# Loading x in quadrant order with transfers that write all 128 partitions

## The reference

```python
xn = _layernorm(x, axis=-1)
# the network, for all 16384 tokens
s = jnp.einsum('btd,dm->btm', xn, Win) + bin_          # D = 512, M = 64
h = jax.nn.relu(s[..., None] * W1 + b1)                # 16 hidden values for each of the 64
g = jnp.einsum('btmh,mh->btm', h, W2) + b2
out = jnp.einsum('btm,md->btd', g, Wout) + bout
# the result
x = x + attention(xn, ...) + out
```

## Time and profile before

| | before |
|---|---|
| median of 3 runs | 382.41 us |
| the three runs | 381.01 to 385.93 us |
| profiled execution | 379.16 us |
| its span (first to last instruction) | 377.4 us |
| PE, DVE, POOL, ACT busy | 83%, 74%, 63%, 58% |
| queue of SP, packets' time as a share of 16 engines | 78.0% |
| moved by DMA | 89.89 MB, 238 GB/s over the span |
| granted TensorE clock, mean | 0.93 |

### The profile page before, as it was taken

How to read it: one execution, slowest core, us unless ns; L and a number is a source line. 1 busy time by engine, 2 the same in 40 slices (tenths; PEclk the granted TensorE clock), 3 DMA queues, 4 the chain that set the end, 5 groups by cost and what they waited for, 6 DMA issues and landing times.

```text
span 377.4 us, 5029 instructions
## 1 busy us (share of the span) xinstructions
PE 312.2 (83%) x1772; PEld 145.4 (39%) x1772; DVE 280.2 (74%) x426; ACT 219.6 (58%) x270; POOL 237.7 (63%) x209
## 2 busy tenths in 40 slices
PE   2576279979979999999799999989779794997952
PEld 1334054445424634453344443424243342432310
DVE  0759955689899899979999899769549583855332
ACT  2112357555757765757677688877538671787500
POOL 8336960582973969397684968978571949179500
PEclk9996779999989999999999999999969997999875
DMA  8999939798457898869488797969699997723634
GB/s 215 256 304 368 224 123 213 265 283 231 164 245 194 318 212 320 224 233 302 135 329 206 280 263 236 266 231 267 189 307 226 303 244 254 304 111 159 190 145 188
DMA packets 53512, 89.89 MB, mean 238 GB/s; under 512 B 5720, under 2 KB 38640, under 8 KB 49392
## 3 DMA queue, kind: packets, MB, share of 16 engines
q1 hardware_dynamic: 52640, 89.16, 78.0%
q0 software_dynamic: 640, 0.16, 0.6%
q10 hardware_dynamic: 208, 0.26, 0.3%
HBM read 55.87 MB, written 33.69 MB: 237 GB/s over the span
## 4 chain that ended last, share of the span: by engine, by line
PE 41%; DVE 26%; DMA 22%; issue 5%; SPq 3%; ACT 1%; POOL 1%; DVEq 0%; POOLq 0%
PE op L499 13%; DMA out_dram<-x 12%; DVE x L869 7%; PE s L445 7%; PE g L482 6%; DMA x<-in_L_attn_x_dram 5%; DVE stats L896 5%; DMA xq<-in_L_attn_x_dram 4%; PE T L432 4%; DVE xqT L879 3%; PE rep L466 3%; PE op L326 2%; DVE w2s L745 2%; DVE WvT L821 2%; DVE SL L890 1%
## 5 line engine op out<-in xcount | busy, mean ns | idle before, releaser
L1003 POOL TENSOR_TENSOR x<-x,bias_row 128x512 f32<-128x512 f32 x128 | 163.5, 1316 | 7.3 <-DVE bias_row L736 7.3
L627 ACT ACTIVATE H<-rep,b1c,w1c 128x1024 f32<-128x1024 f32 x128 | 146.5, 1215 | 31.0 <-PE rep L466 19.2
L869 DVE TENSOR_TENSOR x<-x,op 128x1024 f32<-128x1024 f32 x64 | 77.5, 1211 | 40.2 <-PE op L499 37.2
L896 DVE BATCH_NORM_STATS2 stats<-x 128x6 f32<-128x512 f32 x128 | 80.5, 678 | 23.0 <-DMA x<-in_L_attn_x_dram 23.0
L499 PE MATMUL op<-wout,G 64*128 64x512 f32 x256 | 83.8, 733 | 9.4 <-DVE x L869 9.3
L987 POOL TENSOR_TENSOR rstd<-veps,nhalf 128x8 f32<-128x8 f32 x16 | 26.3, 1647 | 87.6 <-DVE veps L906 87.5
L602 ACT ACTIVATE xT<-T 128x512 f32<-128x512 f32 x64 | 38.4, 600 | 65.4 <-PE T L432 65.1
L432 PE MATMUL T<-ident,x 128*128 128x128 f32 x256 | 45.5, 305 | 23.4 <-DMA x<-in_L_attn_x_dram 20.1
L482 PE MATMUL g<-H,w2s 128*32 128x512 f32 x512 | 63.7, 607 | 0.0
L445 PE MATMUL s<-xT,win 128*64 128x512 f32 x128 | 60.5, 617 | 3.6 <-DVE xqT L879 3.6
L445 PE MATMUL s<-xqT,winq 128*64 128x512 f32 x128 | 60.5, 617 | 0.0
(11 more groups left out here) (160 smaller groups left out, 268.2 us busy)
## 6 DMA issues: line engine op xcount, KB each, us to landing
x<-in_L_attn_x_dram SPq DMA_DIRECT2D x32, 1024.0 KB, 7.0
out_dram<-x SPq DMA_DIRECT2D x32, 1024.0 KB, 5.2
xq<-in_L_attn_x_dram SPq DMA_DIRECT2D x64, 256.0 KB, 8.2
x<-in_L_attn_Wq_dram SPq DMA_DIRECT2D x1, 1024.0 KB, 10.2
x<-in_L_attn_Wk_dram SPq DMA_DIRECT2D x1, 1024.0 KB, 13.2
x<-in_L_attn_Wv_dram SPq DMA_DIRECT2D x1, 1024.0 KB, 5.0
x<-in_L_attn_Wo_dram SPq DMA_DIRECT2D x1, 1024.0 KB, 5.5
bias_row<-in_L_ffn_bout_dram SPq DMA_DIRECT2D x1, 256.0 KB, 10.5
```

Of the source, the lines that this page charges most:

```text
L627: act.activation(Hr[half][k % len(Hr[half])][:, :], rep_ps[:, :], ACT.Relu, bias=b1c[:, half, k:k + 1], scale=w1c[:, half, k:k + 1]).then_ ...
L869: dve.tensor_tensor(both, both, o_ps[:, :].rearrange("p (h d) -> p h d", h=2), ALU.add).then_inc(add_done, 1)
L896: dve.bn_stats(stats[:, j, :], x_sb[m][:, j * D:(j + 1) * D]).then_inc(bn_done, 1)
L1003: pool.tensor_tensor(x_sb[m][:, c], x_sb[m][:, c], bias_row[:, :], ALU.add).then_inc(xc_done, 1)
```

## The change

Pairs 0 and 1 are loaded as before. From pair 2 on, `load_quads` issues 16 transfers in place of 4. Before, transfer i took column block i of all 512 tokens to the 32 partitions from 32 i on (256 KB, 512 pieces of 512 bytes). Now transfer t takes all four column blocks of the 32 tokens from 32 t on to all 128 partitions (64 KB, 128 pieces of 512 bytes). The pieces are the same 2048 of 512 bytes, the bytes land in the same places, and the count that DVE waits for is adapted. The four lists that place the side chain are new too.

```diff
-            3, 39, 44, 44, 64, 64, 64, 64, 64, 66, 68, 68, 68, 70, 70, 73, 73, 74, 74, 74, 75, 77, 79, 98, 101, 103,
+            3, 39, 44, 44, 64, 64, 64, 64, 64, 66, 68, 68, 68, 70, 70, 73, 73, 74, 74, 74, 75, 79, 79, 96, 98, 100,
...
@@ -236,18 @@
         def load_quads(n):
             if n > 1:
                 sp.wait_ge(tq_done, 2 * (n - 1))
-            for i in range(DC):
-                sp.dma_start(xq[n % 2][i * QD:(i + 1) * QD, :].rearrange("p (t d) -> p t d", d=P), xq_v[n, 1, i, :, :, :]).then_inc(ldq[n % 2], 16)
+            if n < 2:
+                for i in range(DC):
+                    sp.dma_start(xq[n][i * QD:(i + 1) * QD, :].rearrange("p (t d) -> p t d", d=P), xq_v[n, 1, i, :, :, :]).then_inc(ldq[n], 16)
+            else:
+                for t in range(BLK // QD):
+                    sp.dma_start(xq[n % 2][:, t * P:(t + 1) * P], xq_v[n, 1, :, :, t, :]).then_inc(ldq[n % 2], 16)
...
             if h == 0:
-                dve.wait_ge(ldq[n % 2], 16 * DC * (n // 2 + 1))
+                dve.wait_ge(ldq[n % 2], 16 * (DC + BLK // QD * (n // 2)))
```

More of the change, by code:

```diff
@@ L188, in residual_block @@
         AT_PE = iter((
-            3, 39, 44, 44, 64, 64, 64, 64, 64, 66, 68, 68, 68, 70, 70, 73, 73, 74, 74, 74, 75, 77, 79, 98, 101, 103,
-            105, 107, 109, 111, 132, 141, 143, 162, 165, 167, 169, 173, 175, 201, 203, 205, 207, 225, 226, 232, 237,
-            258, 261, 265, 268,))
+            3, 39, 44, 44, 64, 64, 64, 64, 64, 66, 68, 68, 68, 70, 70, 73, 73, 74, 74, 74, 75, 79, 79, 96, 98, 100,
+            101, 103, 104, 108, 111, 137, 139, 141, 143, 161, 162, 168, 173, 194, 197, 200, 202, 205, 207, 226, 230,
+            239, 257, 261, 265,))
         AT_ACT = iter((
-            40, 41, 45, 46, 65, 69, 69, 70, 72, 72, 72, 103, 104, 108, 134, 139, 161, 166, 168, 194, 199, 204, 224,
-            228, 238, 257, 262, 266,))
+            40, 41, 45, 46, 65, 69, 69, 70, 72, 72, 72, 100, 102, 104, 130, 135, 140, 160, 164, 174, 193, 200, 203,
+            224, 232, 238, 257, 264,))
         AT_DVE = iter((
[3 rows of a table removed]
[3 rows of a table added]
         AT_POOL = iter((
-            -32, 8, 103, 103, 133, 167, 195, 226, 231,))
+            -32, 8, 103, 103, 129, 162, 167, 200, 230,))
         def reach(steps, n, place):
```

## The result

The change takes 454.18 us (median of 4 runs, 452.72 to 456.24) against 381.71 us. The ratio is 1.194, 95% interval 1.184 to 1.205. Direction and mechanism came as forecast; the size did not: 531 us was predicted, and 454.18 lies just under the low end of the range, 455. Executions of these kernels come in a faster and a slower kind: every median here is over all runs, every ratio over the fast ones alone, so a ratio is not quite that of the medians.

What follows compares the result with a forecast made beforehand. PE is close to the limit; SP's queue paces the last bodies and, after the change, every body. 67.1 us to the loop + 15 + 382 + 65.3, plus 1.8 around the span, gives 531 us, range 455 to 590.

Steps and rivals of the forecast that it cites:

- The engines: Quadrant transfers from pair 2 on: source's outermost count 4 puts each on the same four DMA engines; forecast's chance 0.81.
- Ahead of the loop: Before the main loop: quadrant loads of pairs 2 and 3 lengthen, 11 us of the first hidden; adds 15 us (11 to 18).
- DVE's wait: DVE waiting for quadrants: they are issued two bodies (60 us) ahead, so a 20 us load shows no stall there.
- Behind the loop: From the last x loads to the end: compute and stores of the last pairs stay at 65.3 us.
- Twelve bodies: Main loop: 12 bodies at 31.8 us take 382 us (337 to 426) in place of 244.9.
- Price of a quadrant load: One quadrant load on four engines, 262 KB each at 13.4 to 16.7 GB/s: 15.7 to 19.5 us.
- A body: One main-loop body, paced by SP's queue of x, stores and quadrants: 28.1 to 35.5 us, middle 31.8.
- small gap: In a body's sum: gaps shrink to the start-up of an x load, 2.4 us, giving 28.1 us a body.
- full gap: In a body's sum: the 6.0 us of gaps in the last bodies' 20.9 us stay, giving 31.7 to 35.5 us.
- All 16 engines: Rival for quadrant loads: all engines write 128 partitions at 267 to 423 GB/s, about 374 us, 1.5% less; chance 0.10.
- Pieces in series: Rival for quadrant loads: four engines move pieces one after another at 45 ns, 23.2 us a load, 628 us; chance 0.05.
- SP's issuing: Rival in the first eight bodies: above 0.52 us an issue the store is late, 16 us, 395 us in all; chance 0.04.

Runs made afterwards that it cites:

- shares of 2, 4 and 8: The change's 16 transfers with the source's outermost count set to 2, 4 or 8: DMA shares of 14.4, 28.8 and 57.5%; ratios 1.633, 1.200 and 1.030 against before.
- k = 16: The change's 16 transfers to 128 partitions, reading other pieces of x so the source's outermost count is 16: 378.96 us, ratio 1.000 against before.
- k = 2: The change's 16 transfers to 128 partitions, reading other pieces of x so the source's outermost count is 2: 616.69 us, ratio 1.633 against before.
- the reordered kernel: The kernel before, with SP's second store of pair n - 3 moved ahead of the quadrant load of pair n + 2: 360.77 us, ratio 0.948.

## Why the prediction was right in kind and wrong in size

**The engines.** "Cutting both sides alike at the outermost level gives four shares": shown by the shares of 2, 4 and 8.

**Ahead of the loop.** Predicted 15 us. The x loads that open the loop are issued at 82.37 instead of 67.11 us, 15.3 later. The size came right by luck, since the first of the two loads was to cost nothing and cost 6.9 us. A piece of the change's chain from 48 to 66 us, down to SP's line for Wo:

```profile
49.44 4.89 DMA xq<-in_L_attn_x_dram
54.36 1.25 DVE xqT L883
...
61.52 0.38 SPq L249
```

The load of pair 2 lands at 54.3 us, DVE waits 5.8 us for it (the prediction had DVE's wait not show), and behind its turn and PE's transposes of line 330 SP sends Wo at 61.52 instead of 54.61, 6.9 later. From there to the x loads it takes 20.9 us instead of 12.5, 8.4 more, where the second load was to cost 15.

**Behind the loop.** Predicted 65.3 us. From 388.66 to 454.5 us are 65.8.

**Twelve bodies.** Predicted 382 us, 31.8 a body; measured 388.66 - 82.37 = 306.3 us, 25.5 a body. 75.7 of the 77 us that the prediction missed are in this term, and two of its inputs failed. The prediction had named the first itself: "If four engines carry them but the time is under 480 us, the rate of an engine was the wrong term".

The first is "*Price of a quadrant load*". I took the rate of an engine, 13.4 to 16.7 GB/s, from stretches in which 16 engines wrote 32 partitions, and carried it over to four engines that write to 128. That rate belonged to the crowded destination and not to the engine. The Trainium skill, quoted for the rival ("SBUF — State Buffer", section "Door 1: The DMA port swizzle"), says that 32 partitions reach half of the ports, and the rows of before agreed; yet I used the rate under that limit for a case without it. With four engines at work each moves 21.5 GB/s, so a load takes 262 KB / 21.5 = 12.2 us and not 15.7 to 19.5. I had an outer bound from the large pieces, 9.9 us; the truth is nearer to it than to my middle.

The second is "*A body*". With 12.2 us in my formulas, a body is 10.0 + 2.4 + 12.2 = 24.6 us with the small gap and 20.9 - 4.9 + 12.2 = 28.2 with the full one, 26.4 in the middle; the measured 25.5 lies there. The full gap did not stay, since the second store flows on the 12 other engines while four still carry quadrants. The change from 358 to 359 us shows both at once:

```profile
DMA packets 232, 0.32 MB, mean 325 GB/s; under 512 B 4, under 2 KB 174, under 8 KB 232
```

174 - 4 = 170 pieces of 512 bytes in 1 us are 42.5 on each of four engines, their full rate, and the 58 pieces of 4096 bytes that a store moves beside them must be on others. With the one rate corrected, the sum would have been 67.1 + 15 + 12 x 26.4 + 65.3 + 1.8 = 466 us; the rate is thus 65 us of the miss and the gap about 11.

**The rivals.** All 16 engines: not what the change does; with k = 16 the last four bodies did gain 7.9 us (I had 4 to 10), but lost as much before, 378.96 us in all where I had 374. Pieces in series: refuted, 23.7 ns apart and not 45. SP's issuing: with 0.55 us an issue, just over my limit of 0.52, 16 of them cost nothing measurable, 382.30 us; with the 0.65 us of k = 16 the first eight bodies were 2.6 us longer, not 16.

**What was to be seen.** Right: SP held over 10 us by a full queue, PE waiting for x, late stores. Wrong: 86 GB/s and not 54 to 67, x loads 26 us apart and not 28 to 36, PE 73% busy and not near 60%.

## What to carry to other kernels

Before a transfer is recut, write down the outermost count of both sides: here a source that steps through 4 blocks ran on 4 DMA engines, though the destination had 128 partitions. Take a resource's rate from a stretch in which that resource is the limit; a rate read under sharing says nothing about the case without it. And put what is needed last behind what is waited for first: moving one store ahead of a prefetch in the same queue was worth 5.2% here, more than any recut of the prefetch that I tried.

## What the runs showed of the hardware that I had not expected

With 2, 4 or 8 engines at work, a DMA engine moves 512-byte pieces at 23.7 ns each, 21.5 GB/s, close to the 26 GB/s of an engine with pieces of 4 and 8 KB; with all 16 and 128 partitions it is 18.8. The small pieces cost a fifth to three tenths, not a half; the half came from writing 32 partitions.

Two queues whose transfers of 32 partitions go to different halves of the partitions reach 306 GB/s, where one queue that serves the halves one after the other stays at 215, be it SP's or ACT's.

The granted TensorE clock, mean over the span, fell from 0.93 to 0.85 in the change and 0.76 with k = 2, and rose to 0.95 in the reordered kernel, with 1.00, the upper of its two levels, from 212 to 294 us, where PE had no idle time. PE's busy share in these kernels is 83%, 73%, 54% and 85%: the clock is lower where PE idles more. In the change PE's busy time grew as the clock fell, from 312.2 to 332.5 us for the same 1772 matmuls. PE's part of the chain there is 9%, so little of this can be in the time.
